# Exact attention scores in two halves of TensorE's rows, with the order of work rewritten around them

## The reference, cut to what matters

```python
x = x + tanh(g_xattn) * xattn(layernorm(x), ctx)   # cross attention to 120 keys, softmax over exact float32 scores
h = layernorm(x)
q, k = rms(heads(rms(h) @ wq.T)) * qn, rms(heads(rms(h) @ wk.T)) * kn   # root per head: rsqrt(mean(x*x) + eps)
a = h + softmax(causal(q @ k.T / sqrt(8))) @ v @ wo.T     # first 32 features stay unchanged
xf = rms(a)
moe = sum over the 2 best of 4 experts of weight * expert(xf)   # experts: gelu, silu and linear layers, then a "down" layer
x = x + tanh(g_ffn) * (a + moe)
```

## Time and profile before

| | |
|---|---|
| three runs | 1074.19, 1075.44, 1075.52 us |
| the profiled execution, its own time | 1072.52 us |
| its span from first to last instruction | 1070.7 us |
| mean granted TensorE clock | 0.987 |
| TensorE matmul busy | 1004.9 us (94%) |
| VectorE busy | 789.2 us (74%) |
| ScalarE busy | 736.1 us (69%) |
| GpSimd busy | 337.8 us (32%) |

### The profile page before, as it was taken

One profiled execution on the slowest core, in us unless ns is written; L12 is line 12 of the kernel. 1 busy time (PEld: TensorE's weight loads), 2 busy tenths in 40 slices (PEclk: granted clock), 3 DMA queues, 4 the chain that ended last, 5 costly groups with the idle time before them and its releaser, 6 DMA issues.

```text
span 1070.7 us, 26205 instructions
## 1 busy us (share of the span) xinstructions
PE 1004.9 (94%) x8649; PEld 626.3 (58%) x8649; DVE 789.2 (74%) x2172; ACT 736.1 (69%) x1334; POOL 337.8 (32%) x463
## 2 busy tenths in 40 slices
PE   6678799999999999999999999999999999999898
PEld 5445456566665656666565666656566665655565
DVE  8667777877787787778778777877877777774723
ACT  6466677676777767677776767777676777767453
POOL 5615134051513405151240515124051512404130
PEclk9989899999999999999999999999999999999999
DMA  7433432233343233434323343432234343221200
GB/s 233 134 106 130 136 112 93 90 102 127 115 142 111 90 92 103 127 115 140 109 92 92 106 127 115 136 109 93 90 111 127 115 135 109 82 67 62 69 1 20
DMA packets 77317, 114.28 MB, mean 107 GB/s; under 512 B 7776, under 2 KB 40160, under 8 KB 77152
## 3 DMA queue, kind: packets, MB, share of 16 engines
q1 hardware_dynamic: 76800, 111.53, 33.0%
q10 hardware_dynamic: 480, 2.26, 0.6%
HBM read 58.97 MB, written 53.74 MB: 105 GB/s over the span
## 4 chain that ended last, share of the span: by engine, by line
PE 64%; DVE 15%; ACT 11%; issue 7%; DMA 1%; SPq 1%; POOL 0%; DVEq 0%; ACTq 0%
PE ps_pv L1362 9%; PE ps_w L1388 9%; PE ps_s2a L1341 7%; PE ps_s2b L1341 5%; PE ps_s2a L1400 5%; PE ps_s2b L1407 4%; PE ps_t L1224 4%; ACT probs L951 4%; PE ps_w L1407 3%; DVE mpadB L1091 3%; PE ps_w L1273 3%; DVE mpadA L1091 3%; PE ps_t L1375 2%; PE ps_w L1224 2%; PE ps_w L1305 2%
## 5 line engine op out<-in xcount | busy, mean ns | idle before, releaser
L951 ACT ACTIVATE probs<-ps_s2a 120x512 f32<-120x512 f32 (+1 forms) x256 | 153.4, 599 | 73.1 <-PE ps_s2a L1341 64.7
L1091 DVE TENSOR_REDUCE mpadB<-ps_w 128x4 f32<-128x512 f32 x240 | 148.8, 684 | 24.9 <-PE ps_w L1305 24.9
L1091 DVE TENSOR_REDUCE mpadA<-ps_w 128x4 f32<-128x480 f32 x224 | 131.5, 651 | 38.0 <-PE ps_w L1305 38.0
L951 ACT ACTIVATE probs<-ps_s2b 120x512 f32<-120x512 f32 (+1 forms) x256 | 153.6, 600 | 0.0
L818 POOL TENSOR_SCALAR_AFFINE_SELECT probs<-probs 128x1024 f32<-128x1024 f32 x128 | 139.8, 1092 | 0.0
L1388 PE MATMUL ps_w<-W,hid 128*128 128x96 f32 x976 | 122.5, 279 | 1.0 <-DVE split_k L985 0.9
L1388 PEld LDWEIGHTS ps_w<-W,hid 128*128 128x128 f32 x976 | 114.9, 193 | 10.4 <-issue 4.9
L786 POOL TENSOR_TENSOR rB<-vrB,neg_half 128x4 f32<-128x4 f32 x16 | 16.1, 1007 | 207.2 <-DVE veB L978 207.2
L1341 PE MATMUL ps_s2a<-qdA,kstA 128*120 128x512 f32 x128 | 68.7, 537 | 7.0 <-ACT probs L951 3.1
L1400 PE MATMUL ps_s2a<-hid,W 128*128 128x512 f32 x152 | 74.4, 604 | 0.0
L1120 DVE SCALAR_TENSOR_TENSOR ym<-ps_w,gates,ym 128x96 f32<-128x96 f32 x184 | 45.7, 311 | 38.5 <-PE ps_w L1388 38.5
(11 more groups left out here) (279 smaller groups left out, 2166.7 us busy)
## 6 DMA issues: line engine op xcount, KB each, us to landing
scratch_Aq<-split_q SPq DMA_DIRECT2D x48, 256.0 KB, 2.4
qdA<-scratch_Aq SPq DMA_DIRECT2D x64, 192.0 KB
scratch_Bq<-split_q SPq DMA_DIRECT2D x48, 256.0 KB, 2.4
scratch_Bk<-split_k SPq DMA_DIRECT2D x48, 256.0 KB, 2.9
qdB<-scratch_Bq SPq DMA_DIRECT2D x64, 192.0 KB
kstB<-scratch_Bk SPq DMA_DIRECT2D x64, 192.0 KB
scratch_Ak<-split_k SPq DMA_DIRECT2D x48, 240.0 KB, 2.3
kstA<-scratch_Ak SPq DMA_DIRECT2D x64, 180.0 KB
```

Source lines behind the costliest of these rows:

```text
L951: nc.scalar.activation(probs[0:k, slot_of(part, *index), :], bank[0:k, :], ACT.Exp, scale=SCALE if part == "A" else 1.0).then_inc(done, 1)
L1091: nc.vector.tensor_reduce(pair[:, :, c, b % 2] if halves else mneg[p][:, :, c, b], bank[:, 0:HT * k].rearrange("p (h k) -> p h k", h=HT), ...
```

## The change

An exact pair of packs becomes four matmuls of 256 columns: rows 0 to 48 of the array hold two heads of a pack and a row of maxima, rows 64 to 112 the two others. Both halves write at the same time into different banks: s2a gets the first two heads of both packs, s2b the last two. The wait before a pair is now for both banks. `qd` shrinks to half; loads and stores of rows follow. The value products of a sequence can be issued in two halves (`early_values`, `late_values`), the downs 0 and 3 in two halves too (`head`, `rest`), and the written order puts these between the exact pairs. The head root becomes exp(-ln(x)/2) on ScalarE, and VectorE's reciprocal goes.

```diff
+def early_values(part, b):
+    return values(part, b, 0, PACK)
+def late_values(part, b):
+    return values(part, b, PACK, NT)
+HEADED = (0, 3)
+def head(e):
+    return one("M", "head", e, None)
+def rest(e, ring="w"):
+    return fill("M", "down", e, ring)
+def down(e, ring="w"):
+    return (head(e) if e in HEADED else []) + rest(e, ring)
 def self_attention():
-    return (one("N", "load", 0, None) + one("N", "ctx", 0, None) + exact("D", 0, 0) + one("B", "hT") + down(1) + exact("D", 0, 2)
-            + one("B", "qk", 0) + one("B", "qk", 1) + one("B", "qk", 2) + one("B", "qk", 3)
-            + exact("D", 1, 0) + estimate("A", 0) + exact("D", 1, 2)
-            + one("B", "squares", 0, None) + values("D", 0)
-            + exact("D", 2, 0) + estimate("A", 1) + exact("D", 2, 2)
-            + values("D", 1) + one("B", "sums", 0, None) + down(0)
-            + exact("D", 3, 0) + one("D", "oT", 0, "t") + estimate("A", 2) + exact("D", 3, 2)
-            + one("A", "base", 0, None) + values("D", 2) + one("D", "nT", 0, "t") + one("B", "root", 0, None))
+    return (one("N", "load", 0, None) + one("N", "ctx", 0, None) + exact("D", 0, 0) + one("B", "hT") + down(1)
+            + exact("D", 0, 2) + one("B", "qk", 0) + one("B", "qk", 1) + early_values("D", 0)
+            + exact("D", 1, 0) + one("B", "qk", 2) + one("B", "qk", 3) + late_values("D", 0)
+            + exact("D", 1, 2) + one("B", "squares", 0, None) + estimate("A", 0) + early_values("D", 1)
+            + exact("D", 2, 0) + head(0) + late_values("D", 1)
+            + exact("D", 2, 2) + rest(0) + one("D", "oT", 0, "t") + one("B", "sums", 0, None) + estimate("A", 1)
+            + exact("D", 3, 0) + early_values("D", 2) + one("D", "nT", 0, "t") + late_values("D", 2)
+            + exact("D", 3, 2) + one("A", "base", 0, None) + one("B", "root", 0, None))
 def second_experts():
-    return (fill("M", "e2_l2", 0) + one("D", "wo", 0, "t") + one("B", "scale", 0, None) + fill("M", "e2_l2", 1)
-            + estimate("A", 3) + values("D", 3) + fill("M", "e3_up", 0) + one("D", "oT", 1, "t") + fill("M", "e3_up", 1)
-            + one("N", "stats", 0, None)
-            + one("D", "nT", 1, "t") + one("A", "mT") + fill("M", "e2_l3", 0) + one("N", "norm", 0, None) + one("D", "wo", 1, "t")
-            + one("D", "out", 0, None) + one("B", "qT") + one("B", "kT") + one("D", "squares", 0, None)
-            + fill("M", "e2_l3", 1, "w"))
+    return (one("D", "wo", 0, "t") + early_values("D", 3) + fill("M", "e2_l2", 0) + one("B", "scale", 0, None) + estimate("A", 2)
+            + late_values("D", 3) + fill("M", "e2_l2", 1) + estimate("A", 3) + fill("M", "e3_up", 0) + one("D", "oT", 1, "t")
+            + fill("M", "e3_up", 1) + one("N", "stats", 0, None) + one("A", "mT") + fill("M", "e2_l3", 0) + one("D", "nT", 1, "t")
+            + one("B", "qT") + one("B", "kT") + one("N", "norm", 0, None) + one("D", "wo", 1, "t")
+            + one("D", "out", 0, None) + one("D", "squares", 0, None) + fill("M", "e2_l3", 1, "w"))
 def cross_attention():
-    return (exact("A", 0, 0) + one("B", "v") + down(2) + exact("A", 0, 2) + one("N", "xT")
-            + exact("A", 1, 0) + estimate("B", 0) + exact("A", 1, 2)
-            + one("D", "norm", 0, None) + one("B", "init", 0, None) + one("B", "copy", 0, None) + values("A", 0)
-            + exact("A", 2, 0) + estimate("B", 1) + exact("A", 2, 2)
-            + values("A", 1) + down(3) + one("M", "store", 0, None) + one("D", "xfT")
-            + exact("A", 3, 0) + one("A", "oT", 0, "t") + estimate("B", 2) + exact("A", 3, 2)
-            + values("A", 2) + one("D", "logits") + one("A", "nT", 0, "t"))
+    return (exact("A", 0, 0) + one("B", "v") + down(2) + exact("A", 0, 2) + one("N", "xT") + estimate("B", 0)
+            + exact("A", 1, 0) + values("A", 0) + one("D", "norm", 0, None) + one("B", "init", 0, None) + one("B", "copy", 0, None)
+            + exact("A", 1, 2) + head(3) + early_values("A", 1)
+            + exact("A", 2, 0) + rest(3) + one("M", "store", 0, None) + estimate("B", 1)
+            + exact("A", 2, 2) + late_values("A", 1) + one("D", "xfT")
+            + exact("A", 3, 0) + one("A", "oT", 0, "t") + early_values("A", 2) + estimate("B", 2)
+            + exact("A", 3, 2) + one("D", "logits") + late_values("A", 2) + one("A", "nT", 0, "t"))
...
-        qd = {p: sb("qd" + p, [P, HT, NT, TOK], F32R) for p in "AB"}
+        qd = {p: sb("qd" + p, [P, HT // 2, NT, TOK], F32R) for p in "AB"}
...
-                        nc.scalar.activation(hr[:], hs[:], ACT.Sqrt, bias=rms_eps[:, 0:1], scale=1.0 / HD).then_inc(root_ready, 1)
+                        nc.scalar.activation(hl[:], hs[:], ACT.Ln, bias=rms_eps[:, 0:1], scale=1.0 / HD).then_inc(log_ready, 1)
+                        act.wait_ge(log_ready, g + 1)
+                        nc.scalar.activation(hr[:], hl[:], ACT.Exp, scale=-0.5).then_inc(root_ready, 1)
...
                         dve.wait_ge(root_ready, g + 1)
-                        nc.vector.reciprocal(hr[:], hr[:]).then_inc(hr_ready, 1)
-                        dve.wait_ge(hr_ready, g + 1)
...
-                        for bk, v in st.drains([], key):
-                            pe.wait_ge(drained[bk], v)
-                        o = bank[0:k, :].rearrange("p (h q) -> p h q", h=HT)
-                        mm(o, kst[p][:, c, b * k:(b + 1) * k], qd[p][:, :, c, b * P:(b + 1) * P],
-                           start=True, stop=True).then_inc(done, 1)
+                        if c % 2:
+                            continue
+                        tiles = [(part, "s2", (b, c + half)) for half in range(2)]
+                        for tile in tiles:
+                            for bk, v in st.drains([], tile):
+                                pe.wait_ge(drained[bk], v)
+                        for cc in range(2):
+                            for half in range(2):
+                                rows = slice(half * HALF_ROWS, half * HALF_ROWS + M_ROW + 1)
+                                o = psum[st.bank[tiles[half]]][0:k, cc * 2 * P:(cc + 1) * 2 * P].rearrange("p (h q) -> p h q", h=2)
+                                ins = mm(o, kst[p][rows, c + cc, b * k:(b + 1) * k], qd[p][rows, :, c + cc, b * P:(b + 1) * P],
+                                         start=True, stop=True)
+                                if cc:
+                                    ins.then_inc(filled[st.bank[tiles[half]]], 1)
```

77 lines of the change are left out of this document (39 added, 38 removed).

## The result

The changed kernel takes 1219.01 us, the median of four runs (1208.48 to 1230.35), against 1074.82 us for the kernel before beside it (1073.59 to 1075.52). The ratio is 1.131, with a 95% interval of 1.121 to 1.141; it leaves out the run of 1230.35, which stands more than 1.5% above the kernel's fastest. The forecast was 1105 us with a range of 1040 to 1126: the direction was right, the size was far off and outside the range. The profiled execution took 1208.48 us, its span is 1206.8 us (before: 1072.52 and 1070.7), and the mean granted TensorE clock fell from 0.987 to 0.922.

A forecast was written before the change was run, and what follows sets the result against it. TensorE's order was taken to bind. Per iteration -4.6 + 0.8 + 0.5 + 1.5 + 2.4 + 1.7 = +2.3 us, over 13.5 iterations +31, ramp -1: 1103 us profiled, median about 1105, range 1040 to 1126.

The forecast's parts named there:

- The pair: TensorE's 16 exact pairs per iteration: 0.41 us each plus entering costs, starts from 12.5 to 7.9 us, -4.6 us.
- What TensorE's other work pays: Value products and downs cut in two: more leavings of split arrays 0.7, repeated weights 0.1, together +0.8 us per iteration.
- A1, B1, B0: TensorE's waits ahead of these estimates in the new order: +0.5, +1.5 and +2.4 us per iteration, in that order.
- the walk: New order laid out engine by engine with traced times: waits of 6.1 us per iteration (0.5 + 1.5 + 2.4 + 1.7).
- the small waits: Waits at pairs, masked products, estimate A3, mT and logits: 2.5 us, less 0.8 that go, +1.7 us per iteration.
- The root: Log and exp replacing square root and reciprocal: 0 on the path, taken from a range of 0 to +1.3 us per iteration.
- estimate A3 0.2: One of the small waits in the new order, ahead of this estimate on TensorE: 0.2 us per iteration.
- The sum at full clock: All terms of a loop iteration added: +2.3 us, all of it in cross attention, giving an iteration of 64.9 us.
- The clock: TensorE's clock in the loop: read as always full, 2.4 GHz level, in one iteration; no term for a fall.
- Ramp and tail: Steps outside the loop: ScalarE sets the pace in both forms, and halved `qd` saves a clearing in the ramp, -1 us.
- the third: Rival: halves don't run side by side, pair 0.75 us, or one more table load for the log; 1133 us, chance 0.10.

The follow-up runs named there:

- e6: The kernel before with the new order alone, keeping whole matmuls and the square root: 1155.8 us, ratio 1.075.
- e1: The changed kernel with the log left out of the root, exp alone, so the root's values differ: 1202.1 us, no ratio given.
- e2: The changed kernel with the old square root and reciprocal put back, new order and halves kept: 1227.2 us, ratio 1.143.
- e7: The changed kernel with dummy matmuls on TensorE before estimates A3 (7), B0 (10), B1 (4) and A1 (2): 1185.8 us, ratio 1.105.
- e10: The kernel before, with only the first matmul of an exact pair now waiting for both banks: 1103.0 us, ratio 1.026.
- e5: The changed kernel's halves in the order of the kernel before, with its square root and uncut products and downs: 1120.6 us, ratio 1.041.
- e11: e7 with its dummies in ramp and tail too, and two more between the bank waits of each pair there: 1201.0 us, ratio 1.118.
- e3: The changed kernel with dummy matmuls on TensorE, ten before estimate A3 and fourteen before B0: 1232.1 us, ratio 1.148.
- e9: e5 with two dummy matmuls between the two bank waits of the second pairs of sequences 1 and 2: 1113.8 us, ratio 1.038.

## Why the prediction failed, by its own steps

- **The pair: right as far as it goes.** 0.43 us where 0.41 was forecast. The 16 pairs' starts add up to 7.7 us per iteration, from 12.5; the forecast was 7.9. So -4.8 was measured where -4.6 was forecast. But by e6 some 2 us of it come from the order alone.
- **What TensorE's other work pays: this step failed.** Forecast +0.8, for cut products and downs. Measured +4.2 (table of e6). The order alone adds 2.0: the products go from 8.0 to 8.8, as forecast, but the queries and keys' matmuls, which are now cut by products, from 1.5 to 1.9, and more beside them. The halves add 2.2: 0.5 by the layer that no longer overlaps with the first A pair, and the rest since what stands behind a pair takes some 0.1 us longer. The forecast had the price of leaving a split array inside the pair's 0.41 and nothing behind it.
- **A1, B1, B0: right in place and releaser, each a little shorter.** A1 idles 0.74 us (forecast 1.0), B1 1.25 (1.5), B0 2.12 (2.7), each released by VectorE's `ym`. B0 starts 9.75 us after qT, where the walk had 9.9. Of the small waits less came than the 1.7 forecast. That cross attention grew by just the forecast 2.3 is in part luck: its waits were shorter and its other work dearer than forecast.
- **The root: this step failed.** "So 0 on the path", and among the small waits "estimate A3 0.2". The measured wait is 2.15 us per iteration. The prediction did see that A2 and A3 follow the root's product; it had the wrong number of table loads ahead of that product. It counted none, with +1.3 for one as its bound, and there are two, one for the log and one for the exp, 2.6 us. With none (e1) A3 doesn't wait at all, as forecast; the order has made this path critical, since even the old root with its one load and reciprocal leaves 1.5 (e2, e6), where in the old order A2's reductions stood ahead of the product. I also took the lower end without a row for it. The Trainium skill (ScalarE: Activation LUTs; Table sets: the hidden batching unit) says that log and exp share a set. This trace disagrees: 16 loads of 1283 ns ahead of the 16 logs and 16 ahead of the 16 exps; the measurement decides.
- **The sum at full clock.** Forecast: pairs -4.6, other work +0.8, waits +6.1, together +2.3. Measured by the table: pairs -5.1, other work +4.2, idle +6.5, together +5.6. The total of the waits was near by luck: A3 brought 2.0 more, and the others together 1.5 less. The 3.3 us missed are, over 13.5 iterations, 45 of the 105 us.
- **The clock: a term put at nothing, and this step failed too.** The prediction read the full clock in the loop and carried it over to a kernel to which it added idle times of 1 to 2.7 us. That cost 33.6 us in the loop's eleven whole iterations, and e7 gives 33.4 of them back. The granted clock of each stretch was in the profile; that it depends on how TensorE is fed was there to see in the ramp, where the old kernel too had half-rate time. The Trainium skill (TensorE: Matmul & The Clock Gate; A second HAM failure mode: psum-queue depth-cycling) describes a kernel that cycles through PSUM banks and whose clock oscillates because TensorE idles shortly and often between groups of matmuls. This trace agrees in kind, with longer idle times of 2.1 us: of the 15 intervals between `yb` products 11 had half-rate time, 2 before.
- **Ramp and tail: wrong sign.** Forecast -1, measured +18.6 ahead of the first `yb`. In the ramp pairs stand close together and wait for both banks: e10 shows 8 us of it with whole matmuls; halves in the old order (e5) 14; the new order with whole matmuls (e6) 11. Part of it is the clock: ahead of the first `yb` the half-rate time rose from 13.7 to 51.9 us. Outside the eleven iterations it rose by 67 us, which would cost some 24 us if it cost there what it did in the loop (33.6 for 92); that is an estimate, and e11's dummies did not win it back.

In short: that the kernel gets slower, and where most waits stand, was forecast rightly and for the reasons that the trace shows; how much slower was not. The clock and the dearer work around the halves were in no rival either. Of the rivals none came. The nearest was the third, "the halves don't run side by side ... or a table load more", by its second part, with 1133.

Left open: why the halves bring the clock down at idle times that whole matmuls bear (e2 against e6). Their load on the array differs in rows, in columns and in the number of matmuls at once, they wait for both banks, and no run varies these one at a time. Why the matmuls behind a split pair take longer isn't shown either. Nor is it known which idle time will trigger a fall, or how long it lasts: the iterations of one execution with the same idle times differ from 68.2 to 78.6 us.

## What to carry to other kernels

A faster instruction on the binding engine is worth only what its neighbours and the banks leave of it. Here 4.8 us saved per iteration in pairs bought nothing: the matmuls behind a split pair got slower by most of what the halves had won, a pair now waits for two banks, and the order that was to separate pairs put estimates right behind what frees their banks. So time a new instruction together with the one behind it. When an order is rewritten, walk it for every engine's queue, and look for the chain that it makes critical (here the root). And a new idle time of 1 to 3 us on TensorE has two prices, the wait and the clock after it: put both in the sum, and take an activation function that the trace hasn't shown with a table load of its own on either side.

## What the runs showed of the hardware

- In the loop the granted clock fell to the 1.2 GHz level behind some idle times of 2.1 us (after, B0 and A3), of 1.25 us (e3, B1) and, with half matmuls, behind one of 1.02 or two of 0.58 and 0.47 us in a row (e5). Dummies in the idle times kept it at 2.4 GHz throughout the loop (e7, e9). With whole matmuls idle times of up to 0.85 us brought no fall in the loop (e10), and those of 2.35 us six short ones (e6: 24 us at half rate in eleven iterations, against 130 in e2 with half matmuls and 2.11 us).
- A log between exps costs two table loads of 1283 ns, one before it and one before the exp behind it; before the gelus there is a third.
- Two matmuls of 49 rows and 256 columns on separate rows of the array start within 0.01 us, the next round follows after 0.22 us, and the whole pair takes 0.43 us, 0.12 less than two whole matmuls of 512 columns. The four matmuls of 256 columns behind it then take 1.06 us and not 0.96 (after, e6).
